# Softmax scales as rows: a DRAM scratch and two small transfers in place of TensorE transposes, and the merge one step on

## What is computed

```python
q, k, v = (to_heads(q), to_heads(k), to_heads(v))          # 16 heads of 64
weight = jnp.einsum('bhld,bhnd->bhln', q * scale, k * scale)
full_mask = jnp.concatenate([mask, jnp.ones((b, l), dtype=bool)], axis=1)
weight = jnp.where(full_mask[:, None, None, :], weight, neg)
weight = jax.nn.softmax(weight.astype(jnp.float32), axis=-1)
out = jnp.einsum('bhln,bhnd->bhld', weight, v)
return out.transpose(0, 2, 1, 3).reshape(b, l, heads * dim_head) @ Wout
```

## Time and profile before

| | |
|---|---|
| median of 3 runs | 892.66 us |
| the profiled execution | 892.87 us, span 891.1 us |
| granted PE clock | 0.995 of full speed |
| busy: PE, DVE, ACT, POOL | 851.9, 579.7, 437.5, 349.0 us |
| DMA | 183.04 MB, q1 busy 57.8% of 16 engines |

### The profile page before, as it was taken

The page is one execution under the profiler, slowest core; times in us unless marked ns, Lnnn a source line. Parts: engine busy times, 40 slices in busy tenths (PEclk is TensorE's granted clock), DMA queues, the critical chain, the costliest instruction groups (busy, mean ns, idle before and its releaser), DMA issues.

```text
span 891.1 us, 17432 instructions
## 1 busy us (share of the span) xinstructions
PE 851.9 (96%) x6353; PEld 794.7 (89%) x6353; DVE 579.7 (65%) x1540; ACT 437.5 (49%) x1017; POOL 349.0 (39%) x362
## 2 busy tenths in 40 slices
PE   3899999999999999999999999999989999998997
PEld 2889999999999999999999999999967789987885
DVE  7445555566576878756566666777767546746885
ACT  4465554545546455544646454455425224334552
POOL 5634523645353664745454453413211110003442
PEclk9999999999999999999999999999999999999999
DMA  6365336457566677575666755887578366842310
GB/s 200 95 221 172 120 130 224 177 192 231 197 237 239 242 234 272 200 236 195 234 215 213 238 192 191 292 336 246 207 295 329 136 257 262 352 143 89 101 48 25
DMA packets 71109, 183.04 MB, mean 205 GB/s; under 512 B 6336, under 2 KB 19568, under 8 KB 65008
## 3 DMA queue, kind: packets, MB, share of 16 engines
q1 hardware_dynamic: 70928, 181.90, 57.8%
q10 hardware_dynamic: 96, 0.02, 0.0%
HBM read 130.00 MB, written 50.86 MB: 203 GB/s over the span
## 4 chain that ended last, share of the span: by engine, by line
PE 81%; DVE 10%; issue 3%; ACT 3%; DMA 2%; POOL 1%; SPq 0%; DVEq 0%; ACTq 0%; POOLq 0%
PE pJ L1621 15%; PE pJ L1622 14%; PE pJ L1623 14%; PE pV L1751 8%; PE pS L1729 4%; PE pT L1737 3%; PE pS L1737 3%; PE pT L1729 2%; PE pS L1621 2%; PE pS L1622 2%; PE pS L1623 2%; PE pX L1652 1%; DVE late L1578 1%; DMA WS<-w_split 1%; PE pV L1621 1%
## 5 line engine op out<-in xcount | busy, mean ns | idle before, releaser
L1621 PE MATMUL pJ<-WV,XT 128*128 128x256 f32 x544 | 159.2, 293 | 0.0
L1622 PE MATMUL pJ<-WV,XT 128*128 128x256 f32 x544 | 154.5, 284 | 0.0
L1623 PE MATMUL pJ<-WV,XT 128*128 128x256 f32 x544 | 154.4, 284 | 0.0
L848 ACT ACTIVATE SP<-SP,xneg 128x768 f32<-128x768 f32 (+1 forms) x96 | 85.8, 895 | 119.5 <-DVE xneg L1200 119.5
L1621 PE MATMUL pJ<-XT,WK 128*128 128x384 f32 (+1 forms) x384 | 126.9, 330 | 3.9 <-DVE VT L1096 2.9
L1623 PE MATMUL pJ<-XT,WK 128*128 128x384 f32 (+1 forms) x384 | 125.2, 326 | 0.0
L1622 PE MATMUL pJ<-XT,WK 128*128 128x384 f32 (+1 forms) x384 | 125.1, 326 | 0.0
L1096 DVE TENSOR_TENSOR KT<-pJ,KT 128x384 fp32r<-128x384 f32 x96 | 51.1, 535 | 90.8 <-ACT KT L825 90.3
L1621 PEld LDWEIGHTS pJ<-WV,XT 128*128 128x128 f32 x544 | 104.8, 193 | 0.5 <-issue 0.2
L1622 PEld LDWEIGHTS pJ<-WV,XT 128*128 128x128 f32 x544 | 104.9, 193 | 0.0
L1623 PEld LDWEIGHTS pJ<-WV,XT 128*128 128x128 f32 x544 | 104.8, 193 | 0.0
(11 more groups left out here) (374 smaller groups left out, 2171.5 us busy)
## 6 DMA issues: line engine op xcount, KB each, us to landing
WS<-w_split SPq DMA_DIRECT2D x14, 2048.0 KB, 8.9
WV<-wv_split SPq DMA_DIRECT2D x20, 1024.0 KB, 7.0
WK<-wk_split SPq DMA_DIRECT2D x40, 512.0 KB, 4.4
w_split<-wkst SPq DMA_DIRECT2D x40, 512.0 KB, 3.3
w_split<-wvst SPq DMA_DIRECT2D x40, 512.0 KB, 3.8
XA<-w_split SPq DMA_DIRECT2D x4, 2048.0 KB, 12.9
xraw<-in_ctx SPq DMA_DIRECT2D x7, 768.0 KB, 6.4
wk_split<-WK SPq DMA_DIRECT2D x8, 512.0 KB, 3.8
```

Source lines behind the costliest of these rows:

```text
L848: ac.activation(SP[:, I % 2, h, 0:w], SP[:, I % 2, h, 0:w], ACT.Exp, bias=xneg[:, I % 2, h:h + 1], scale=XSC, accum_out=total).then_inc(c_ ...
L1621: te.matmul(dst, a(HI), b(HI), start=start, stop=False)
L1622: te.matmul(dst, a(HI), b(LO), start=False, stop=False)
L1623: return te.matmul(dst, a(LO), b(HI), start=False, stop=stop)
```

## The change

PE's transposes of the scales and ACT's copies of them go. In their place ACT issues DMAs: write_scales writes a column of alpha or linv (256 numbers, each a piece of 4 bytes) to a scratch in DRAM as a row; spread_scales reads the row back, broadcast to all partitions, into scl. alpha is written at the end of the step that makes it, linv behind the high halves of the probabilities, and the broadcast is issued after the exponentials. alpha and linv now lie in one tile, scales. The merge of step I moves into step I + 1, ahead of the masked maximum, when I is in rounds 1, 2, 4 or 5; in the last step it stands behind the join of the step before.

```diff
+        scd = nc.dram_tensor("scale_rows", [2, 2 * 2 * P], F32).ap()
-            def scale_rows(I):
+            def spread_scales(I):
...
+                n = R % SPLITS
+                act.wait_ge(d_row[m % 2], row_count(m))
                 if m > 0:
                     act.wait_ge(c_mg, I)
...
+                act.dma_start(scl[:, 0:n, :, :].rearrange("p s h t -> p (s h t)"),
+                             scd[I % 2, 0:2 * P * n].partition_broadcast(P)).then_inc(d_scl, 16)
+
+            def write_scales(I, s):
+
+                m = I - (I // PAIRS // SPLITS + 1) * PAIRS
+                if s == 0 and m >= 2:
+                    act.wait_ge(d_scl, 16 * (m - 1))
+                act.wait_ge(*((c_alpha, m + 1), (c_rec, pair_index(I) + 1))[s])
+                act.dma_start(scd[I % 2, 2 * P * s:2 * P * s + 2 * P].rearrange("(h p) -> p h", p=P), scales[:, I % 2, s, :],
+                              allow_slow_non_contiguous=True).then_inc(d_row[m % 2], 16)
...
                         prob_hi(I, h, q)
+                if I // PAIRS % SPLITS == 2:
+                    write_scales(I, 1)
...
-                scale_rows(I)
...
                     rescale(n)
+                    if n // PAIRS % SPLITS:
+                        write_scales(n, 0)
+                spread_scales(I)
...
             def merge(I):
-                dve.wait_ge(c_scl, m + 1)
+                dve.wait_ge(d_scl, 16 * (m + 1))
...
                 prob_lo(I, 1, 1)
+                if I > 0 and (I - 1) // PAIRS % SPLITS:
+                    merge(I - 1)
...
-                merge(I)
+                if I // PAIRS % SPLITS == 0:
+                    merge(I)
...
+                if I == ITERS - 1:
+                    merge(I)
...
-            def rows_of_scales(I):
...
-                rows_of_scales(I)
                 if n < ITERS:
                     scores(n, 0)
```

More of the change, by code:

```diff
@@ L102, in perceiver_layer @@
         xneg = sb("xneg", [P, 2, 2])
-        alpha = sb("alpha", [P, 2, 2])
+        scales = sb("scales", [P, 2, 2, 2])
         nmr = sb("nmr", [P, 4])
-        linv = sb("linv", [P, 2, 2])
         rs = sb("rs", [P, 2, 2])
@@ L175, in perceiver_layer @@
         ROWS = (slice(0, DH), slice(DH, P))
+        alpha, linv = scales[:, :, 0, :], scales[:, :, 1, :]
         BANK = (pS[:, 0, :], pS[:, 1, :], pT[:, 0, :], pT[:, 1, :])
@@ L203, in perceiver_layer @@
         c_s = sem("c_s"); c_ttr = sem("c_ttr"); c_neg = sem("c_neg"); c_exp = sem("c_exp"); c_alpha = sem("c_alpha")
-        c_lu = sem("c_lu"); c_rec = sem("c_rec"); c_rb = sem("c_rb")
+        c_lu = sem("c_lu"); c_rec = sem("c_rec"); d_row = (sem("d_row"), c_lrstd); row_count = lambda m: 16 * sum(1 + i // PAIRS % 2 for i in range(m % 2, m + 1, 2)) + 2 * (m % 2)
         c_t = sem("c_t"); c_th = sem("c_th"); c_tl = sem("c_tl"); c_o = sem("c_o")
-        c_of = sem("c_of"); c_scl = sem("c_scl"); c_mg = sem("c_mg")
+        c_of = sem("c_of"); d_scl = sem("d_scl"); c_mg = sem("c_mg")
         c_os = sem("c_os"); c_oh = sem("c_oh"); c_ol = sem("c_ol")
@@ L382, in steps_of @@
             return None
[L384 to L392, removed]
         @block.sync
@@ L858, in rescale @@
                     act.wait_ge(c_lu, m - 1)
-                    act.wait_ge(c_rb, m - 1)
+                    act.wait_ge(d_row[m % 2], row_count(m - 2))
                 for h in range(2):
@@ L870, in scale_rows @@
                 m = I - (R // SPLITS + 1) * PAIRS
-                act.wait_ge(c_rb, m + 1)
+                n = R % SPLITS
+                act.wait_ge(d_row[m % 2], row_count(m))
                 if m > 0:
                     act.wait_ge(c_mg, I)
-                if R % SPLITS == SPLITS - 1 and pair_index(I) > 0:
+                if n == 2 and pair_index(I) > 0:
                     act.wait_ge(c_of, pair_index(I))
-                w = 256 if R % SPLITS == 1 else 512
-                ac.activation(scl[:, :, :, :].rearrange("p s h t -> p (s h t)")[:, 0:w], pX[:, 0:w], ACT.Copy).then_inc(c_scl, 1)
+                act.dma_start(scl[:, 0:n, :, :].rearrange("p s h t -> p (s h t)"),
[7 more added lines that the diff above has]
+                              allow_slow_non_contiguous=True).then_inc(d_row[m % 2], 16)
             def prob_hi(I, h, q):
@@ L1216, in sums @@
                     dve.wait_ge(c_lu, m + 1)
+                    if m >= 2:
+                        dve.wait_ge(d_row[m % 2], row_count(m - 2))
                     ve.reciprocal(linv[:, par, :], lsum[:, cols]).then_inc(c_rec, 1)
@@ L1753, in outputs @@
                     last.then_inc(c_o, 1)
-            def rows_of_scales(I):
[L1757 to L1769, removed]
-                        last = te.transpose(pX[:, 256 + L * h:256 + L * h + L], linv[:, par, h:h + 1].broadcast_to([P, P]), ident[:, :])
-                last.then_inc(c_rb, 1)
             def latent(k):
```

3 lines of the change are left out of this document (removed).

## The result

The changed kernel takes 1140.17 us (median of 4 runs, 1130.95 to 1145.04), the kernel before beside it 893.01 us (4 runs, 890.71 to 897.21): a ratio of 1.275, 95% interval 1.265 to 1.284. The forecast was 909 us with a range to 926. The direction was right, the size off by 231 us. The profiled execution has a span of 1139.6 us at a granted PE clock of 0.902 (0.995 before).

What follows compares the result with a forecast made beforehand. PE bounds the kernel (busy 96% of the span, 81% of the chain). 892.9 - 10.5 (transposes) + 20.3 (merge and late ACT) + 1 (rounds 1 and 4) + 5 (end) = 908.7, said as 909 us; range 886 to 926 us.

Steps and rivals of the forecast that it cites:

- Transposes removed: Between PE's value and score matmuls: 0.43 us gained in 16 steps with four transposes, 0.22 in 16 with two, 10.5 us.
- Issues on ACT: After the alpha activations, ACT issues the write (0.52 us) and broadcast (0.43 us) before the next high half, making it late.
- D: ACT's lateness from the two DMA issues ahead of VT's or KT's high half: 1.1 us, bounds 0.7 to 1.4.
- the rival of cheap issues: An issue holds ACT for much less than its row shows, D = 0.2 us: 895 us in all; chance 0.12.
- The merge and D on PE: Main loop, rounds 2 and 5: moved merge and late ACT make PE wait 2.9 us in each of 7 step pairs, 20.3 us.
- The transfers: Row writes and broadcasts land just in time for the merge (4.6 us of room), and WK's fetch isn't hurt: 0 us.
- WK is fetched a step ahead of its need: SP's later wait for c_of delays the WK fetches queued behind it, but there is a step to spare: 0 us.
- late transfers: Rival: broadcasts take 6.4 us, 1.8 us late in 7 even steps and about 1 us in 8: +20 us, 928; chance 0.14.
- part 2: The prediction's part on ACT's two DMA issues ahead of hand-overs to PE; one issue bounded at 0.26 to 1.40 us.
- The end: End of the attention part: the last merges and joins come later, and PE's third projection starts near 668.7: +5 us.

Runs made afterwards that it cites:

- experiment 3: The changed kernel with each write's 256 pieces of 4 bytes replaced by 16 pieces of 64 bytes (scales wrong, waits and order kept): 938.38 us, ratio 1.049.

## Why the prediction was wrong

**1. Transposes removed (10.5 us gained): right.** The distance from the value job to the scores in round 5 is now 0.21 us:

```profile
804.07 0.28 PE L1635 MATMUL pJ<-WV,XT 128*128 128x256 f32 x1
804.28 0.79 PE L1739 MATMUL pS<-KT,Q 64*128 64x384 f32 x6
```

**2. Issues on ACT (D = 1.1 us): right.** From alpha's start to VT's high half it is 1.54 us (307.44 to 308.98) against 0.37 us, so D = 1.17 us. The rows of the issues are 0.37 and 0.43 us at the median, so the rival of cheap issues is out. The 50 ns that the Trainium skill gives (page DMA: Bandwidth & Descriptors, "Where the ~2 µs actually goes") stand in its account of a DMA issued from GpSimd; ACT's issues here take seven to nine times as long.

**3. The merge and D on PE (20.3 us): right in size where it can be seen.** It can't be in the changed kernel, where the stalls cover it. In experiment 3 the waits for VT and KT are 18.6 + 3.5 = 22.1 us, 3.4 us of which the kernel before has too (2.9 + 0.5): 18.7 us more, for which the forecast had 7 x (1.7 + 0.9) = 18.2 us. That the sums agree so well is luck: the forecast had 7 waits of 1.7 us for VT and 7 of 0.9 us for KT, all in rounds 2 and 5, and the run has 18 of 1.0 us for VT, some in the other rounds, and 7 of 0.5 us for KT.

**4. The transfers (0 us): this step failed, twice.** It asked only whether the two transfers land before their own reader comes ("I count it as just hidden, 0 us"), and never what they do to the others. The second 0 us in it fell with that, "WK is fetched a step ahead of its need": PE waits 64 us for WK. The 4-byte pieces cost 202 us in all, 1140.17 against 938.38, their own late landings included; what they do to the other transfers alone is 176 us in the kernel before with unwaited writes. The landing times then fail too: taken as within 4.6 us from transfers of 3.3 and 6.4 us, they are over 10 us and 14.8 us in the steps shown above. With larger pieces the outputs still wait 18.7 us, mostly for late broadcasts, where the "late transfers" rival had +20 us. That rival was right in kind for the smaller part of this term; its size agrees by luck, as it had 15 steps of 1 to 1.8 us and one wait of 7.45 us makes more than a third. The larger part had no rival at all. "No row shows a 4-byte scatter" stood in part 2, but only its issue was bounded there; what it does after its issue had no bound.

**5. The end (+5 us): half.** From the start of the last outputs matmul to the third projection it was 652.1 to 663.75, 11.6 us; in experiment 3 it is 693.5 to 707.72, 14.2 us: 2.6 us more.

With the terms as measured in experiment 3 the sum is 892.9 - 10.5 + 18.7 + 18.7 + 2.6 = 922.4 us, where that run took 938.38. The 16 us between were not taken apart. PE's lower granted clock after waits can be most of them: by an estimate from the two granted clocks, (1 - 0.982) x 936.5 - (1 - 0.995) x 891.1 = 12 us at most, as part of the slow stretches is waiting. The forecast had no term for it.

The range to 926 us misses even experiment 3 by 12 us, and the kernel by 214: its upper end came from waits alone, and no wait bounds what a transfer does to its neighbours.

## What to carry to other kernels

When a change adds a transfer of a shape that the trace doesn't have, bound two things apart: when it lands for its reader, and what it does to the transfers already there; for the second, its bytes and its share of the queue say nothing (0.8% of the engines' time cost 20% of the kernel's). A column of 4-byte numbers written as an adjoining row in DRAM is such a shape: make the pieces 32 bytes or more (laid 64 bytes apart they are cheap to write too, but then they don't form one row to be read back), or keep the matmul transposes, which here cost an estimated 10.5 us in all, less than any version with transfers lost. The sign to look for is a queue with the same packets and bytes and more engine time than before.

## What the runs showed that I had not expected

- Adjoining 4-byte pieces to DRAM: 3.7 us of the kernel's time for each write of 128 or 256, with nothing waiting for it; packets of other transfers of up to 10 us where 2.2 us was the longest before. Pieces of 8 bytes 0.8 us, of 16 bytes 0.15 us, of 32 bytes nothing. The same pieces 64 bytes apart: nothing to 0.3%.
- A broadcast from one partition of SBUF: about 0.4 us for a packet of 1 KB and 7.4 us to landing of 128 KB, against about 0.09 us (packets of 1 and 2 KB) and 4.1 us from a row in DRAM.
